# A GNN with two attention layers: tile rows gathered once into a ring, node blocks resident, edge sums in halves

## The reference, cut to what matters

```python
def gatv2_layer(x, src, dst, Wl, Wr, att, bias, n_nodes, heads):
    xl = (x @ Wl).reshape(N, heads, Dh)
    xr = (x @ Wr).reshape(N, heads, Dh)
    e = leaky_relu(xl[src] + xr[dst], 0.2)
    logits = einsum('ehd,hd->eh', e, att)
    m = segment_max(logits, dst)
    a = exp(logits - m[dst])
    alpha = a / segment_sum(a, dst)[dst]
    out = segment_sum(alpha[:, :, None] * xl[src], dst)
    return out.mean(axis=1) + bias
```

## Time and profile before

| | |
|---|---|
| median of 3 runs | 4050.35 us (4050.16 to 4050.52) |
| the profiled execution, its span | 4048.7 us |
| set-up and preparing block of layer 1 | 0 to 189 us |
| edges of layer 1 (first transposes to last sums of TensorE) | 198 to 1838 us |
| edges of layer 2 (the same) | 2095 to 3481 us |
| neighbour sums (first product of the counts) and dense layers | from 3607 us |

### The profile page before, as it was taken

One profiled execution on the slowest core, in us unless ns is written; L12 is line 12 of the kernel. 1 busy time (PEld: TensorE's weight loads), 2 busy tenths in 40 slices (PEclk: granted clock), 3 DMA queues, 4 the chain that ended last, 5 costly groups with the idle time before them and its releaser, 6 DMA issues. The chain is left out here.

```text
span 4048.7 us, 76266 instructions
## 1 busy us (share of the span) xinstructions
PE 3293.6 (81%) x24199; PEld 2204.4 (54%) x24199; DVE 2807.3 (69%) x6887; ACT 1717.6 (42%) x3696; POOL 2796.9 (69%) x2157
## 2 busy tenths in 40 slices
PE   0399999999999999996339977777777777568986
PEld 0246666666666666674226655554455555346763
DVE  3558888888888888886537755565555555579972
ACT  3254444444444444432215433333333333147861
POOL 4488888888777777505678888888888885537630
PEclk9999999999999999986669988888888888569997
DMA  2233343343333333323114433333333332211210
GB/s 58 51 65 80 86 88 86 86 89 85 80 87 86 86 85 88 75 54 83 48 36 79 91 74 67 68 69 67 67 68 73 69 68 48 52 26 40 44 34 28
DMA packets 607173, 274.68 MB, mean 68 GB/s; under 512 B 445801, under 2 KB 568077, under 8 KB 606260
## 3 DMA queue, kind: packets, MB, share of 16 engines
q1 hardware_dynamic: 261848, 102.14, 11.7%
q0 software_dynamic: 107328, 77.78, 11.1%
q10 hardware_dynamic: 237600, 89.88, 9.1%
HBM read 161.25 MB, written 105.94 MB: 66 GB/s over the span
## 5 line engine op out<-in xcount | busy, mean ns | idle before, releaser
L901 PE MATMUL L_e_ps_z<-L_e_xT,L_w_abs 128*128 128x500 f32 x2700 | 1501.4, 642 | 0.0
L826 POOL DMA_INDIRECT L_e_xs<-in_x_dram,src_idx x880 | 1193.1, 1356 | 335.4 <-issue 261.4
L826 POOL DMA_INDIRECT L_e_xs<-x_d,src_idx x820 | 1079.7, 1317 | 253.3 <-issue 249.8
L952 PEld LDWEIGHTS L_e_ps_v<-L_e_xs,L_e_p 125*128 125x128 f32 x5400 | 860.0, 204 | 628.3 <-issue 569.6
L996 ACT ACTIVATE L_e_rl<-L_e_ps_z 128x500 f32<-128x500 f32 x1350 | 793.0, 587 | 883.0 <-PE L_e_ps_z L901 883.0
L952 PE MATMUL L_e_ps_v<-L_e_xs,L_e_p 125*128 125x65 f32 x5400 | 796.2, 274 | 11.1 <-DVE L_e_acc L1180 9.4
L1180 DVE SCALAR_TENSOR_TENSOR L_e_acc<-L_e_acc,L_e_row,L_e_ps_v 128x130 f32<-128x130 f32 (+1 forms) x1440 | 448.5, 311 | 424.1 <-PE L_e_ps_v L952 281.4
L888 PE MATMUL L_e_ps_x<-ident,L_e_xs 125*64 125x125 f32 x1800 | 288.7, 285 | 310.7 <-DMA L_e_xs<-x_d,src_idx 251.8
L989 ACT ACTIVATE L_e_xT<-L_e_ps_x 128x500 f32<-128x500 f32 x450 | 264.3, 587 | 619.3 <-PE L_e_ps_x L891 590.4
L901 PEld LDWEIGHTS L_e_ps_z<-L_e_xT,L_w_abs 128*128 128x128 f32 x2700 | 427.4, 198 | 77.8 <-issue 24.3
L1163 DVE TENSOR_TENSOR L_e_p<-L_e_ohc,L_e_ae 125x640 f32<-125x640 f32 x540 | 427.1, 818 | 0.0
(11 more groups left out here) (304 smaller groups left out, 3620.2 us busy)
## 6 DMA issues: line engine op xcount, KB each, us to landing
L_v_d<-L_e_acc ACTq DMA_DIRECT2D x225, 260.0 KB
L_e_dlb<-dloc_d SPq DMA_DIRECT2D x90, 468.8 KB, 4.9
L_v_d<-L_e_acc ACTq DMA_DIRECT2D x225, 130.0 KB
L_e_xw<-x_d SPq DMA_DIRECT2D x1800, 12.0 KB
L_e_xs<-in_x_dram,src_idx POOLq DMA_INDIRECT x900
L_e_xs<-x_d,src_idx POOLq DMA_INDIRECT x900
L_e_lim<-limits_d SPq DMA_DIRECT2D x180, 39.1 KB
L_max_d<-L_e_me SPq DMA_DIRECT2D x45, 78.1 KB
```

The source lines that it names most:

```text
L826: pool.indirect_dma_start(xs[c.slot(XR)][:, n, 0:D], None, lay.x_rows, bass.IndirectOffsetOnAxis(k.src_idx[:, u:u + 1], 0)).then_inc(gath[ ...
L901: pe.matmul(ps_z[part % ZR][:, 0:QT], lay.w_abs[:, part * 128:(part + 1) * 128], xT[q][:], start=True, stop=True).then_inc(s["z_ready"], 1)
L952: ins = pe.matmul(ps_v[u // 2 % 2][:, u % 2 * VX + v * XW:u % 2 * VX + (v + 1) * XW], p[st % 3][:, u % NQ, v, :, :].rearrange("e n h -> e ...
```

## The change

Source rows are gathered once per tile (800 gathers, not 900) into a ring `tiles` of 64 tiles, in groups of 16. ACT copies them from the ring to the units' places in `xs` (now a ring of 6 chunks in both layers), one chunk ahead, four units in each step. The node blocks of all 98 windows lie in SBUF for the whole layer (`xw`, one DMA), and TensorE picks a unit's block by a register: it loads the 20 places of a chunk at the end of the chunk before. The product with the one-hot matrix takes 128 columns, the lower 64 of which are overwritten by the transposes that now follow it. Each product of `sums` is split into two of 64 columns, and in each half step two units of sums come first and then half of the projects. Layer 1 has 2 groups (32 tiles) issued ahead, layer 2 has 4 (64 tiles: 2 groups in each of the two blocks). SP's `serve` waits for the tiles that a chunk needs and tells ACT; the list of the next chunk is fetched behind it. The ring of limits and of `dlb` has 2 places in layer 1 and 3 in layer 2, as memory allows.

```diff
+TR = 64
+TF = 16
+NF = G // TF
+RF = TR // TF
+XR = 6
+LR = 8
+FETCHED = (2, 4)
...
-                for b in range(NB):
-                    pool.indirect_dma_start(srcu[:, b * T:(b + 1) * T], ...)
+                    if b < 2:
+                        pool.indirect_dma_start(srcu[:, b * T:(b + 1) * T], ...)
                     pool.indirect_dma_start(dstu[:, b * T:(b + 1) * T], ...)
...
+def counts(eng, name, places):
+    regs = [eng.alloc_register(f"{name}{n}") for n in range(places.shape[1])]
+    eng.load(regs, places)
+    return [(eng.snap(r, donate=True, min_val=0, max_val=63) & 63) + 1 for r in regs]
+
+def fetch_tiles(k, pool, lay, f0, f1):
+    for f in range(f0, f1):
+        if f >= RF:
+            if (f - RF) % 16 == 0:
+                copies = counts(pool, f"{lay.nm}reuse{f}_", k.reuse[0:1, f - RF:min(f + 16, f1) - RF])
+            pool.wait_ge(lay.copied, copies[(f - RF) % 16])
+            pool.sem_inc(lay.freed, 1)
+        for i in range(TF):
+            g = f * TF + i
+            pool.indirect_dma_start(lay.tiles[:, g % TR * D:(g % TR + 1) * D], None, lay.x_rows,
+                                    bass.IndirectOffsetOnAxis(k.src_tile[:, g:g + 1], 0)).then_inc(lay.gath[f % RF], 16)
+            if i == 3 and f > f0:
+                tiles_there(pool, lay, f - 1)
+    tiles_there(pool, lay, f1 - 1)
+
+def tiles_there(pool, lay, f):
+    pool.wait_ge(lay.gath[f % RF], 16 * TF * (f // RF + 1))
+    pool.sem_inc(lay.fetched_to, 1)
+
+def listed(eng, lay, c, row, top):
+    regs = [eng.alloc_register(f"{lay.nm}{row}_{c.number}_{n}") for n in range(CU)]
+    eng.load(regs, lay.lists[c.slot(LR)][0:1, row, :])
+    return [eng.snap(r, donate=True, min_val=0, max_val=top) for r in regs]
+
+def serve(k, sp, lay, c):
+    sp.wait_ge(lay.ld_w[c.slot(2)], c.uses(2) * 16)
+    sp.sem_inc(lay.listed, 1)
+    sp.wait_ge(lay.fetched_to, counts(sp, f"{lay.nm}need{c.number}_", lay.lists[c.slot(LR)][0:1, 2, CU - 1:CU])[0])
+    sp.sem_inc(lay.rows_there, 1)
+    if c.back(-1).there():
+        list_units(k, sp, lay, c.back(-1))
+
+def row_places(act, lay, c):
+    act.wait_ge(lay.rows_there, c.val(1, 1))
+    return listed(act, lay, c, 1, (TR - 1) * D)
+
+def copy_rows(act, lay, c, places, q):
+    for n in range(q, CU, NQ):
+        ins = act.activation(lay.xs[c.slot(XR)][:, n, 0:D], lay.tiles[:, bass.ds(places[n], D)], ACT.Copy)
+    if q == NQ - 1:
+        ins.then_inc(lay.copied, 1)
...
+    lay.xw = sbuf(nc, ctx, lay.nm + "e_xw", [3 * WN, 128 + (NW - 1) * D], BF16)
...
-                load_windows(k, sp, lay, fixed(0))
+                sp.dma_start(lay.xw[:, 128 - D:].rearrange("r (w d) -> r w d", d=D),
+                             bass.AP(k.x3_d.tensor, 0, [[D, 3 * WN], [WN * S3, NW], [1, D]])).then_inc(lay.ld_x, 16)
+                serve(k, sp, lay, fixed(0))
...
-                fetch_rows(k, pool, lay, 0, EARLY if lay.norm else lay.ahead * CU)
+                fetch_tiles(k, pool, lay, 0, 2)
...
+                act.wait_ge(s["ones"], XR + 1)
+                places = row_places(act, lay, fixed(0))
+                for q in range(NQ):
+                    copy_rows(act, lay, fixed(0), places, q)
...
                     for j in range(Q):
                         n = j * NQ + q
-                        pe.transpose(ps[0:D, j * T:(j + 1) * T], xs[r][:, n, 0:D], k.ident[0:T, 0:T])
+                        pe.matmul(ps[:, j * T:(j + 1) * T], xw[:, bass.ds(blocks[n], 128)],
+                                  oht[c.slot(2)][:, n * T:(n + 1) * T], start=True, stop=True)
                     for j in range(Q):
                         n = j * NQ + q
-                        ins = pe.matmul(ps[D:128, j * T:(j + 1) * T], xw[c.slot(3)][:, n, :],
-                                        oht[c.slot(2)][:, n * T:(n + 1) * T], start=True, stop=True)
+                        ins = pe.transpose(ps[0:D, j * T:(j + 1) * T], xs[r][:, n, 0:D], k.ident[0:T, 0:T])
                     ins.then_inc(s["x_ready"], 1)
+
+                def window_blocks(c):
+                    pe.wait_ge(lay.listed, c.val(1, 1))
+                    return listed(pe, lay, c, 0, (NW - 1) * D)
...
                     for v in range(HV):
-                        ins = pe.matmul(ps_v[u // 2 % 2][:, u % 2 * VX + v * XW:u % 2 * VX + (v + 1) * XW],
-                                        p[st % 3][:, u % NQ, v, :, :].rearrange("e n h -> e (n h)"),
-                                        xs[c.slot(XR)][:, u, :], start=True, stop=True)
+                        for half in range(2):
+                            ins = pe.matmul(ps_v[u // 2 % 2][64 * half:64 * half + 64, u % 2 * VX + v * XW:u % 2 * VX + (v + 1) * XW],
+                                            p[st % 3][:, u % NQ, v, WN // 2 * half:WN // 2 * (half + 1), :].rearrange("e n h -> e (n h)"),
+                                            xs[c.slot(XR)][:, u, :], start=True, stop=True)
...
-                    for part in range(4):
-                        if part % (4 // C) == 0 and (c.after(1) or q >= 1) and zc.there():
-                            project(zc, zq, part // (4 // C))
+                    for half in range(2):
                         if c.after(3) and bc.there():
-                            sums(bc, bq, part)
+                            sums(bc, bq, 2 * half)
+                            sums(bc, bq, 2 * half + 1)
+                        if (c.after(1) or q >= 1) and zc.there():
+                            for part in range(C // 2 * half, C // 2 * (half + 1)):
+                                project(zc, zq, part)
+                    if q == NQ - 1 and c.back(-1).there():
+                        blocks[:] = window_blocks(c.back(-1))
...
                     if c.there():
                         copy_xT(c, q)
+                    one = c.back(-1)
+                    if one.there():
+                        if q == 0:
+                            if one.after(XR):
+                                act.wait_ge(s["v_ready"], one.val(CU, CU * (1 - XR)))
+                            places[:] = row_places(act, lay, one)
+                        copy_rows(act, lay, one, places, q)
```

More of the change, by code:

```diff
@@ L81, in __init__ @@
         self.x_node, self.x_rows, self.next_table, self.next_node = x_node, x_rows, next_table, next_node
-        self.v_d, self.max_d, self.norm, self.ahead = v_d, max_d, norm, AHEAD[1 if norm else 0]
-        self.ring = 9 if norm else 6
+        self.v_d, self.max_d, self.norm = v_d, max_d, norm
+        self.fetched = FETCHED[1 if norm else 0]
+        self.slack = 3 if norm else 2
 class Turn:
@@ L305, in _ @@
                 xs.wait()
+                l3.wait()
             @block.gpsimd
@@ L352, in _ @@
                 link(dve.tensor_scalar(w32[:], wcol[:], float(WN), None, ALU.mult))
+                units = Link(dve, s["units"])
+                units(dve.tensor_scalar(turns_i[:], gidx[:], 6, None, ALU.arith_shift_right))
+                units(dve.scalar_tensor_tensor(out=ring_off[:], in0=turns_i[:], scalar=-float(TR), in1=gidx[:],
+                                               op0=ALU.mult, op1=ALU.add))
+                units(dve.tensor_scalar(ring_off[:], ring_off[:], float(D), None, ALU.mult))
+                units(dve.tensor_scalar(need_i[:], gidx[:], 4, None, ALU.arith_shift_right))
+                units(dve.tensor_copy(last_u[:], key_all[0:1, TF - 1:G:TF]))
+                units(dve.tensor_scalar(last_u[:], last_u[:], 2, None, ALU.arith_shift_right))
+                units(dve.tensor_scalar(last_u[:], last_u[:], 205.0, None, ALU.mult))
+                units(dve.tensor_scalar(k.reuse[:], last_u[:], 10, None, ALU.arith_shift_right))
+                for h in range(2):
+                    dve.wait_ge(s["src_turned"], 4 * h + 4)
+                    units(dve.tensor_copy(k.src_tile[:, h * 4 * BLK:(h + 1) * 4 * BLK], ps[4 + h][0:T, 0:4 * BLK]))
+            @block.tensor
+            def _(pe):
+                pe.wait_ge(s["src_f"], 1)
+                for b in range(KT):
+                    c = slice((b % 4) * BLK, (b % 4 + 1) * BLK)
+                    pe.transpose(ps[4 + b // 4][0:T, c], sgf[:, b, :], k.ident[0:BLK, 0:BLK]).then_inc(s["src_turned"], 1)
             @block.gpsimd
@@ L372, in _ @@
                 st.wait()
+                us = Dma(sp, s["unit_store"])
+                sp.wait_ge(s["units"], 4)
+                us.start(k.unit_d[1].rearrange("(b p) -> p b", p=BLK), ring_off[:], elements=True)
+                us.start(k.unit_d[2].rearrange("(b p) -> p b", p=BLK), need_i[:], elements=True)
+                us.wait()
             @block.scalar
             def _(act):
+                act.activation(sgf[:], sg[:], ACT.Copy).then_inc(s["src_f"], 1)
                 for t in range(NT):
@@ L511, in _ @@
                 sp.wait_ge(s["dve3"], NB + 16)
-                st.start(k.win_d.rearrange("(b p) -> p b", p=BLK), k.win_idx[:], elements=True)
+                sp.wait_ge(s["units"], 11)
```

(30 more changed lines are left out.)

153 lines of the change are left out of this document (79 added, 74 removed).

## The result

The changed kernel takes 3855.04 us (median of 4 runs, 3849.69 to 3856.84), the kernel before 4050.26 on the same chip: ratio 0.9521, 95% interval 0.9508 to 0.9535. That is -195 us where -130 was forecast: faster, inside the range of 3840 to 4040 by 15 us, outside the forecast's own range of 3880 to 3960, and past the better rival B (3873). The profiled execution has a span of 3854.8 us against 4048.7: -193.9.

A forecast was written before the change was run, and what follows sets the result against it. Layer 1 was taken as bound by TensorE, layer 2 by the number of gathers. Layer 1's start +27, its chunks -58 and layer 2 -99 gave -130, so 3920 us from 4050; range 3840 to 4040.

The forecast's parts named there:

- rival B: Whole kernel: no stalls on ACT, DVE and the ring, half of POOL's added work; 3873 us, chance 0.14.
- layer 1's start: Set-up, preparing block and first chunks: ACT stops until group 2 is marked, delaying chunk 1; +27 us, ends +5 and +35.
- its chunks: Layer 1, TensorE: chunk period falls from 35.15 to 33.8 us, over 43 chunks -58 us, ends -90 and +215.
- the blocks between the layers: Preparing and tables blocks before layer 2's edges end earlier with fewer gathers: -17 us, ends -25 and -5.
- POOL's additions: Layer 2, POOL: two waits, two increments and three register loads for each of 46 groups; +14 us, ends 4 and 36.
- the ring waits: Layer 2, POOL: waits until an earlier group is copied, where a chunk reaches past a whole group; +10 us, ends 0 and 60.
- The ends: Layer 2: blocks before the edges -17 us; last chunk starts one chunk later after the last gather, +22 us.
- The allowances: Layer 1: ACT's load and copies delay the first relu, +0.5 us a chunk; DVE's fuller period, +0.2.
- C: Layer 1: DVE and a relu behind copies cannot follow, period stays at 35.15 us; 3978 us, chance 0.18.
- D: Register loads on TensorE and ACT: each of twenty costs 0.269 us, layer 1's chunk becomes 42.2; 4380 us, chance 0.07.
- E: TensorE's sums: halves run in series, unit stays at 0.45 us and pauses are added; 4121 us, chance 0.09.
- F: Layer 1, POOL: ring too small, POOL stops 5 us in each of 46 groups, +220; 4140 us, chance 0.04.

The follow-up runs named there:

- Run 7: The changed kernel with one more gather per group of 16 tiles, into a place nobody reads: 3947.98 us, ratio 0.9759.
- Run 3: The kernel before with only the two edits to the sums (halves; two units ahead of each half of the projects): 3990.1 us, ratio 0.9876.
- run 1: The changed kernel with the sums undivided again (one product of 128 columns instead of two of 64), in the new order: 3891.11 us, ratio 0.963.
- Run 8: The changed kernel with each of ACT's copies cut into two of 32 columns, 20 more ACT instructions a chunk: 3884.77 us, ratio 0.9606.
- run 4: The changed kernel with a chunk's 20 places read by 20 one-register loads on TensorE and ACT, instead of one load: 4631.94 us, ratio 1.1452.

## Why the prediction was right

The terms of the sum, forecast and measured: layer 1's start +27 and +14, its chunks -58 and -86, the blocks between the layers -17 and -26, layer 2's edges -82 and -92, and 3 us behind them. What bounds each layer, and so the way to the time, was right. The size was not: every term came out 9 to 28 us lower, which added up to 64 us, half of the forecast again, and the wide range held it.

**Layer 2, gathers.** -128 was 84 x 1.52. Run 7 has 1.50 a gather; the span shows 84 x 1.62 = -136, because the mean spacing stayed. POOL's additions (+14) and the ring waits (+10) were nearly nothing: 11.6 us of waits stand inside the old spacing. **The ends** hid this: the tail grew by 43.8, not 22. Not one but two chunks run behind the last gather (chunks 43 and 44 start 22.3 apart), since with groups of 16 the rows of chunk 43 were in the last group as well, and ACT's wait for them held chunk 42. -136 + 44 = -92, against -82 from my terms (-128 + 14 + 10, and 22): errors of 32 and 22 us, of opposite sign. That these met is luck.

**Between the layers** -26 against -17. The tables block lasts 71.9 instead of 91.5 us from its first POOL instruction to chunk 0 (-19.6, forecast -20). The rest is the drain of layer 1, which a faster TensorE shortens and which I had not counted: from chunk 44's start to the last gather of the merging block 145.8 instead of 154.0, -8.

**Layer 1, TensorE.** The step of 6.32 came out at 6.30. Two of its parts were off and met: the turn took 0.76, not 0.64, and the separate 0.10 ahead of the reduce was not there. And the reason for the gain was in part wrong: of the 0.41 that I took off the step, 0.23 was the turn (0.87 to 0.64) and 0.18 the sums. Run 3 has the sums' edits alone and takes off 0.44 (6.28, against 6.72 from start to start in the earlier trace rows); the new turn on top gives nothing. What each edit is worth does not add up: against the kernel before, undivided sums with the new turn and order save 1.33 us a typical chunk (run 1), halves with the old turn 2.3 in the chunks that wait for no gather (run 3), both together 2.16. That the step met is luck in this part.

**The allowances** were the mis-sized term: +0.5 a chunk for ACT and +0.2 for DVE, together +30 us. The mean chunk fell by 2.00, not 1.35: -86, not -58. TensorE found its next relu done nearly always. Run 8 shows how near it was: 0.34 us a chunk for 20 more instructions. This is why C (the chunk stands still) did not come.

**Layer 1, start.** +27 forecast, +14 measured (chunk 1 at 240.29, against 226.34). The gathers of the edges block begin at 191.3, 7.5 us before chunk 0, and ACT copies the first rows of chunk 1 at 219.1, 20 us after chunk 0's start, where I had put 33; chunk 0 then ran 21 us more, not 26.

**Register loads.** 1.2 us forecast, 1.35 and 1.36 measured, hidden on TensorE. D failed because a load of twenty is 0.068 a register; run 4 shows that by single loads the kernel would have lost 14.5%. My price for that, 8.4 us a chunk, was below the 14 measured: single loads follow each other at 0.39 us on TensorE, not 0.27, and the clock was missing. For layer 2 I had +100; at 8.4 us over chunks of 25, against 28.9 for the gathers, my own numbers make about 200, and run 4 has +172. The Trainium skill (Runtime: NRT & Kernel Launch, "Instruction fetch mechanics") has 200 ns a register even in bulk, for loads that the page's terms call loads from HBM. Here the lists lie in SBUF, and the trace has 1363 ns for twenty, not the 4000 that this figure would give.

**E** failed as the trace of before suggested: sixteen instructions on halves in 0.61 us, where E had 0.45 for each unit's eight. The Trainium skill (TensorE: Matmul & The Clock Gate, "The mechanism") lets loads overlap running matmuls only when the row group differs, though the same section also lets a load into the background weight buffer go ahead. L1058's halves share their rows and lie in two column groups, and the measured 0.61 speaks against the first rule. My sum by it was wrong too: load plus stream at 0.11 make 0.88 a unit, not the 0.45 of E. **F**: a full ring stopped POOL for 0.3 us in layer 2 (107 us in layer 1, where POOL has the time).

## What to carry to other kernels

Splitting a product so that its halves run side by side saves only what is left after what each group costs its neighbours (about 0.25 us here, 0.10 of it the change of shape ahead): gather such products into groups before splitting, and price the group with both neighbours. Measure each of two edits alone before crediting both: here one of them gave nothing beside the other. Where transfers are handed over in groups, count how many consumers stand behind the last group, and who waits for it in front of work that was ready. An engine at 60% can be an instruction away from the path: read the wait in the step where its work is bunched, not its share.
